# Products that nobody reads, in a score bank set aside, in the last ticks of a two-layer attention kernel

## The chip, the cores and the metric

The kernel runs on one core of a Trainium2 chip. The metric is the device time of one execution in microseconds (us); less is better. The median of three runs of the kernel before is 2475.11 us.

## The reference, cut to what matters

Sixteen sequences of 512 rows with 128 features pass through two layers. Each layer is a layer norm, then an attention and a feed-forward block that are added to the same input. The first attention has 16 heads of 64 with a causal mask. The second ("L1") has 8 heads with two score maps each, so 16 maps of 512x512 for a sequence, no mask, 8 features a map, rotary positions, and a norm of each head's result:

```python
xn = _layernorm(x)
x = x + _L0_attn_ref(xn, ...) + _L0_ffn_ref(xn, ...)
xn = _layernorm(x)
x = x + _L1_attn_ref(xn, ...) + _L1_ffn_ref(xn, ...)
# inside _L1_attn_ref
scores = jnp.einsum('bshd,bthd->bhst', q, k) * d ** (-0.25)
w = jax.nn.softmax(scores, axis=-1)
o = o1 - lam * o2
```

## The kernel before, in words

All five engines walk through one list of ticks (`clocks()`). In a tick each engine does the pieces that a fixed table gives it, in an order written out by hand. A sequence's first attention takes 32 ticks; its second attention follows 58 ticks after its start (`L1_AT`), beside the first attention of the next sequence. So TensorE has the products of two sequences at hand in nearly every tick. Three clocks (g for the first half of the work, h for the second half, k for the second half of the last sequence) run together until tick 519 and apart after it (`CLOCKS`). `late(g)` is true from g = 528, when no first attention is left: from there TensorE has only the end of sequence 14's second attention (clock h), the last sequence's projections (g = 528 to 532) and then the last sequence's second attention (clock k, from 538), with nothing of another sequence beside it.

The second attention of a sequence goes in steps of `l1_steps`. A step can hold a "top" (`second_tops`, product at L1768) and a "key" (`second_keys`, product at L1754). Both are a pair of bf16 products with 512 columns, one on the array's rows 0 to 47 (to 50 for keys), one on rows 64 to 111 (to 114), each into a score bank of its own. VectorE takes the row maximum of a top's two banks (`row_max1`, L1362); ScalarE takes the exponential of a key's two banks (`exp1`, L1044). There are 32 tops and 32 keys. The keys lag the tops by 13 steps for the last sequence (`KEY_LAG`), because a key needs the row maxima of its group as extra rows: TensorE turns them (L1739), ScalarE and VectorE split them in three (L1028, L1349 to L1354), and SyncE stores them by DMA (L766). So the last sequence has 13 steps with tops alone, 19 with both and 13 with keys alone. After each 8 keys come the value products of the group (`pv1`, L1721: 16 products in f32, shown as 32 instructions, on all rows of the array and 32 columns each), then the turning of the heads (L1585) and the head norm on VectorE and GpSimd (L1370 to L1393, L852, L854).

The score banks sc0 to sc5 (`SCB = 6`) are dealt in turn, in the order of `score_order()`, by `in_turn`. Before a product TensorE waits until the reader of the tile that had the bank before has read it (`bank_free`). Two further banks (pj0, pj1) serve all other products.

The last sequence's projections for rotary positions: TensorE waits for the layer norm's result, turns it (`xnT1`, L1585), ScalarE copies it (L947), TensorE multiplies it with four weights (`rq`, `rqs`, `rk`, `rks`; L1595), VectorE rotates and splits the results (L1330 to L1342), SyncE stores them (L742) and loads them stacked (L759); the first top waits for that.

Of the kernel before, what the change touches and what calls it, by code (L numbers as in the profile page):

```python
# [22 lines left out]
NB = 16  # L23
T = 512
D = 128
P = 128
# [26 lines left out]
STACK = SLOTS * DS  # L53
# [45 lines left out]
TICKS = 4 * NPAIR  # L99
# [52 lines left out]
VALUES_AT = (8, 8)  # L152
PJB = 2
SCB = 6

def l1_chunk(h, last, part=None):
# [94 lines left out]
def l1_steps(h, k, part=None):  # L252

    steps = []
    for n, clock in enumerate((h, k)):
        if clock is not None:
            i = Seq((clock - L1_AT) // TICKS)
            if i.live() and i.last() == (n == 1):
                steps.extend((i, t) for t in l1_chunk(clock, n, part))
    return steps  # L260
# [114 lines left out]
def score_order():  # L375

    order = []

    def second_keys(h, k, part):

        for i, t in l1_steps(h, k, part):
            if t >= KEY_LAG[i.last()]:
                order.extend(("st1", 2 * (t - KEY_LAG[i.last()]) + n, i.lo) for n in range(2))

    def second_tops(h, k, part):

        for i, t in l1_steps(h, k, part):
            if t < NU:
                order.extend(("mx1", 2 * t + n, i.lo) for n in range(2))

    def tops(g, lag, q):

        p, i = pair(g, lag)
        if i is not None:
            order.extend(("mx0", 6 * p + max(0, 2 * (q - 1)) + j, i.lo) for j in range(2))

    def turned(g, lag, group):

        p, i = pair(g, lag)
        if i is not None:  # L400
            order.extend(("tr0", 6 * p + 2 * group + n, i.lo) for n in range(2))

    for g, h, k in clocks():
        if g is not None and g % TICKS == 0:
            order.append(None)
        r = next(t for t in (g, k, h) if t is not None) % 4
        if late(g) and r == 0:
            second_keys(h, k, 0)
            tops(g, 0, 0)
            second_keys(h, k, 1)  # L410
            second_tops(h, k, 0)
            turned(g, 2, 1)
            second_tops(h, k, 1)
        elif late(g) and r == 1:
            second_tops(h, k, 0)
            turned(g, 2, 2)
            second_keys(h, k, 0)
            second_tops(h, k, 1)
            second_keys(h, k, 1)
        elif late(g) and r == 2:  # L420
            second_tops(h, k, 0)
            second_tops(h, k, 1)
            tops(g, 0, 2)
            second_keys(h, k, 0)
            tops(g, 0, 3)
            second_keys(h, k, 1)
        elif late(g) and r == 3:
            second_keys(h, k, 0)
            second_keys(h, k, 1)
            second_tops(h, k, 0)  # L430
            turned(g, 1, 0)
            second_tops(h, k, 1)
        elif r == 0:
            second_keys(h, k, 0)
            second_tops(h, k, 0)
            turned(g, 2, 1)
            tops(g, 0, 0)
            second_keys(h, k, 1)
            second_tops(h, k, 1)
        elif r == 1:  # L440
            turned(g, 2, 2)
            second_keys(h, k, 0)
            second_tops(h, k, 0)
            second_tops(h, k, 1)
            second_keys(h, k, 1)
        elif r == 2:
            tops(g, 0, 2)
            second_keys(h, k, 0)
            second_tops(h, k, 0)
            second_tops(h, k, 1)  # L450
            second_keys(h, k, 1)
            tops(g, 0, 3)
        else:
            second_keys(h, k, 0)
            second_tops(h, k, 0)
            turned(g, 1, 0)
            second_keys(h, k, 1)
            second_tops(h, k, 1)
    return order

def in_turn(order, banks):

    uses, of_bank, n = {}, [[] for _ in range(banks)], 0
    for use in order:
        if use is None:
            n = 0
            continue
        of_bank[n % banks].append(use)  # L470
        uses[use] = (n % banks, len(of_bank[n % banks]))
        n += 1
    return uses, of_bank
# [3 lines left out]
PJ_USES, _ = in_turn(PJ_ORDER, PJB)  # L477
TILES, TILES_OF = in_turn(score_order(), SCB)

def pj_use(seq, name):

    return PJ_USES.get((name, seq.lo), (0, 0))
# [29 lines left out]
def build_program(nc, a, out):  # L513
    ctx = ExitStack()
    with ctx:
# [52 lines left out]
        mx0 = sb("mx0", [P, NROWS, 8])  # L568
# [17 lines left out]
        QS = sb("QS", [P, H1, T], BF16)  # L586
        KS = sb("KS", [P, H1, T], BF16)
# [22 lines left out]
        pj = [ps(f"pj{n}") for n in range(PJB)]  # L610
        sc = [ps(f"sc{n}") for n in range(SCB)]

# [39 lines left out]
        reader = {"mx0": (s_mxd0, 8 * NPAIR), "tr0": (s_ev, N_TURN), "mx1": (s_mxd1, NS * NT), "st1": (s_exp1, NS * NT)}  # L652
# [918 lines left out]
        def _(pe):  # L1571
            pe.wait_ge(s_ld[0], NLOAD[0])
            used = []

            def bank(i, name):

# [134 lines left out]
            def pv1(i, g):  # L1711

                if g == 0:
                    b_, u = pj_use(i, "vals")
                    pe.wait_ge(s_pje[b_], u)
                t, full = bank(i, f"w{g}")
                for k in range(NT):
                    pe.wait_ge(s_exp1, i.upto(L1N, GS * (NT * g + k + 1)))
                    for j in range(GS):
                        unit = i.upto(NU, (GS * (NT * g + k) + j) // 2)  # L1720
                        last = pe.matmul(t[32 * j:32 * (j + 1), :], values1[i.last()][:, k, (GS * g + j) // 2, :],  # L1721
                                         pt1[:, 2 * (unit % UNITS) + j % 2, :], start=k == 0, stop=k == NT - 1)
                    if k < NT - 1:
                        last.then_inc(s_pv1, 1)
                last.then_inc(full, 1)
# [17 lines left out]
            def second_keys(h, k, part):  # L1743

                for i, t in l1_steps(h, k, part):
                    queries, keys = stacks[i.last()]
                    if (m := t - KEY_LAG[i.last()]) >= 0:
                        group, slot, k, _ = l1_key_pair(m)
                        if m % GU == 0:
                            pe.wait_ge(s_nd[group % 2], i.upto(96, 48 * (group // 2 + 1)))  # L1750
                        for n in range(2):
                            bank_free(i, "st1", 2 * m + n)
                            r = slice(HALF * n, HALF * n + STACK + 3)
                            pe.matmul(sc[tile_bank(i, "st1", 2 * m + n)][:, :], keys[r, slot, P * k:P * (k + 1)], queries[r, slot, :],  # L1754
                                      start=True, stop=True).then_inc(s_st1, 1)

            def second_tops(h, k, part):

                for i, t in l1_steps(h, k, part):
                    queries, keys = stacks[i.last()]  # L1760
                    if t == 0:
                        pe.wait_ge(s_stk, i.upto(64, 64))
                    if t < NU:
                        group, slot, q, _ = l1_max_pair(t)
                        for n in range(2):
                            bank_free(i, "mx1", 2 * t + n)
                            r = slice(HALF * n, HALF * n + STACK)
                            pe.matmul(sc[tile_bank(i, "mx1", 2 * t + n)][:, :], queries[r, slot, P * q:P * (q + 1)], keys[r, slot, :],  # L1768
                                      start=True, stop=True).then_inc(s_mxf1, 1)

            def second_values(h, k, part):

                for i, t in l1_steps(h, k, part):
                    if (group := l1_heads(i, t, VALUES_AT[i.last()])) is not None:
                        pv1(i, group)

            def others(g, h, k):

# [15 lines left out]
                if (i := at(g, XNT1_AT)) is not None:  # L1794
                    if i.first():
                        pe.wait_ge(s_vprep, N_VPREP)
                    pe.wait_ge(s_lnv[1], i.upto(24, 12))
                    transpose4(i, "xnT1", lambda k: xn[:, k, :])
                for w in range(2):
                    if (i := at(g, ROPE_AT[w])) is not None:  # L1800
                        if w == 0:
                            b_, u = pj_use(i, "xnT1")
                            pe.wait_ge(s_pje[b_], u)
                        for c, name in enumerate((("rq", "rqs"), ("rk", "rks"))[w]):
                            project(i, name, lambda k: w_l1[:, 2 * w + c, :], lambda k: xnT1[:, :], 1)
# [192 lines left out]
```

## Time and profile before

| | us |
|---|---|
| median of 3 runs (lowest, highest) | 2475.11 (2465.77, 2478.99) |
| the profiled execution, its own time | 2475.11 |
| its span | 2473.2 |
| TensorE / ScalarE / VectorE / GpSimd busy | 2349.1 / 1876.5 / 1832.7 / 1443.5 |
| TensorE's mean granted clock, share of 2.4 GHz | 0.982 |

The span is what the trace covers; 1.9 us of the profiled execution lie around it. A granted clock of 1.00 is 2.4 GHz, 0.50 is 1.2 GHz. TensorE's busy time counts from a product's start to its modelled end, so products that overlap are counted once, and a product that waits for a bank isn't busy.

### The profile page before, as it was taken

To read this page: it belongs to the slowest core of one execution; us is meant where nothing else is said; L and a number is where in the kernel's file an instruction comes from. 1 tells how busy PE (TensorE), PEld (TensorE's weight loads), DVE (VectorE), ACT (ScalarE), POOL (GpSimd) and SP (SyncE) were. 2 spreads that over 40 slices of the span, in tenths; PEclk is the share of its full clock that TensorE was granted. 3 is DMA by queue.
4 is the path that set the end of the run, shared out by engine and by line. 5 is a ranking of instruction groups with operands and counts; after the bars stand their busy time and mean duration, and the time that the engine had idled before them with its cause. 6 is when DMAs were issued, how large, how long until landed. Compare 5 with 4: busy or idle time off the path is not lost.

```text
span 2473.2 us, 82166 instructions
## 1 busy us (share of the span) xinstructions
PE 2349.1 (95%) x32896; PEld 1136.1 (46%) x32896; DVE 1832.7 (74%) x5637; ACT 1876.5 (76%) x4707; POOL 1443.5 (58%) x1356
## 2 busy tenths in 40 slices
PE   6999999999999999999999999999999999999877
PEld 3554444444544444444444544444444444544322
DVE  5568687787877778687787877778786887877674
ACT  4877877877778787877878777887777877787434
POOL 5975574756648466574756657475574756556201
PEclk9999999999999999999999999999999999999877
DMA  3011020200202020020201102020020201102020
GB/s 100 4 38 23 7 58 3 57 6 20 45 3 62 3 57 8 6 58 3 62 3 29 36 7 57 3 57 7 7 58 3 62 2 40 25 3 57 2 56 5
DMA packets 59946, 70.45 MB, mean 28 GB/s; under 512 B 11056, under 2 KB 55344, under 8 KB 56368
## 3 DMA queue, kind: packets, MB, share of 16 engines
q1 hardware_dynamic: 59568, 65.21, 11.4%
q8 instruction: 262, 4.29, 0.7%
q14 instruction: 116, 0.95, 0.1%
HBM read 35.04 MB, written 29.36 MB: 26 GB/s over the span
## 4 chain that ended last, share of the span: by engine, by line
PE 77%; DVE 16%; ACT 3%; issue 2%; DMA 1%; SPq 0%; POOL 0%; POOLq 0%; DVEq 0%; ACTq 0%
PE pj L1595 18%; PE pj L1691 12%; PE sc L1659 10%; PE pj L1721 10%; PE sc L1676 5%; PE sc L1768 5%; PE pj L1707 5%; DVE mx L1362 5%; PE pj L1615 5%; PE sc L1754 4%; DVE pq L1309 4%; PE pj L1585 3%; ACT pt L1044 1%; DVE y L1330 1%; DVE onrm L1372 1%
## 5 line engine op out<-in xcount | busy, mean ns | idle before, releaser
L845 POOL TENSOR_SCALAR pq<-pq,rsum 128x128 f32<-128x128 f32 (+3 forms) x1024 | 1151.8, 1139 | 772.8 <-DVE rsum L1316 771.2
L1362 DVE TENSOR_REDUCE mx<-sc 128x1 f32<-128x512 f32 x1024 | 644.1, 679 | 247.5 <-PE sc L1768 247.1
L996 ACT ACTIVATE pq<-pq,mx 128x128 f32<-128x128 f32 (+3 forms) x1024 | 569.8, 570 | 25.9 <-DVE mx L1309 25.7
L1044 ACT ACTIVATE pt<-sc 128x512 f32<-128x512 f32 x1024 | 543.9, 607 | 36.0 <-PE sc L1754 34.6
L1309 DVE CUSTOM_DVE_ANT_0 pq<-sc,relkey 128x128 f32<-128x128 f32 (+3 forms) x1024 | 448.5, 484 | 158.7 <-PE sc L1659 156.1
L1014 ACT ACTIVATE pt<-sc 128x512 f32<-128x512 f32 (+1 forms) x768 | 376.6, 535 | 162.3 <-PE sc L1676 159.5
L1659 PE MATMUL sc<-K,Q 64*128 64x128 f32 (+3 forms) x2048 | 362.5, 452 | 15.7 <-DVE mx L1309 9.4
L1691 PE MATMUL pj<-pt,v 128*32 128x512 f32 (+3 forms) x4096 | 303.8, 437 | 8.5 <-DVE y L1330 5.7
L1676 PEld LDWEIGHTS sc<-ident,pq 64*128 64x128 f32 x5120 | 200.1, 138 | 189.8 <-issue 99.7
L1595 PE MATMUL pj<-xnT,wqkv 128*32 128x512 f32 x2048 | 263.1, 606 | 4.0 <-ACT xnT L947 2.0
L1676 PE MATMUL sc<-ident,pq 64*128 64x64 f32 x5120 | 234.6, 227 | 7.4 <-DVE mx L1309 4.0
L1754 PE MATMUL sc<-QS,KS 51*128 51x512 bf16 x960 | 215.7, 383 | 20.4 <-ACT pt L1044 11.9
L1768 PE MATMUL sc<-KS,QS 48*128 48x512 bf16 x960 | 208.5, 385 | 17.4 <-DVE mx L1362 8.5
L1721 PE MATMUL pj<-pt,v 128*32 128x512 f32 x1920 | 224.1, 609 | 0.8 <-DVE y L1330 0.8
L996 ACT ACTIVATION_READ_ACCUMULATOR pq<-pq,mx 128x1 f32 x1024 | 213.1, 208 | 0.0
L1691 PEld LDWEIGHTS pj<-pt,v 128*32 128x32 f32 x4096 | 128.8, 110 | 163.3 <-issue 135.8
L1659 PEld LDWEIGHTS sc<-K,Q 64*128 64x128 f32 x2048 | 156.3, 189 | 80.7 <-issue 28.5
L1768 PEld LDWEIGHTS sc<-KS,QS 48*128 48x128 bf16 x960 | 52.2, 94 | 193.1 <-DVE mx L1362 57.4
L1595 PE MATMUL pj<-wqkv,xnT 128*32 128x128 f32 x4096 | 140.2, 278 | 0.0
L987 ACT ACTIVATE att<-pj 128x512 f32<-128x512 f32 x128 | 76.9, 600 | 74.3 <-PE pj L1691 72.6
L1595 PEld LDWEIGHTS pj<-wqkv,xnT 128*32 128x32 f32 x4096 | 105.5, 111 | 59.3 <-issue 58.2
L1021 ACT ACTIVATE oraw<-pj 128x512 f32<-128x512 f32 x64 | 38.2, 597 | 116.7 <-PE pj L1721 116.7
(117 smaller groups left out, 2836.7 us busy)
## 6 DMA issues: line engine op xcount, KB each, us to landing
scr_p<-y SPq DMA_DIRECT2D x160, 128.0 KB, 2.4
QS<-scr_p SPq DMA_DIRECT2D x30, 384.0 KB, 5.8
KS<-scr_p SPq DMA_DIRECT2D x30, 384.0 KB, 8.5
x_in<-in_L_attn_x SPq DMA_DIRECT2D x16, 256.0 KB, 2.9
scr_p<-tanh SPq DMA_DIRECT2D x32, 128.0 KB, 2.4
out_x<-xres SPq DMA_DIRECT2D x15, 256.0 KB, 2.3
QS<-nrow SPq DMA_DIRECT2D x180, 4.0 KB
wqkv<-in_L_attn_w_qkv SPq DMA_DIRECT2D x1, 1536.0 KB, 6.5
```

Source lines behind the costliest of these rows:

```text
L845: pool.tensor_scalar(rows, rows, rsum[:, row_slot(i, p), c:c + 1], None, ALU.mult).then_inc(s_scl, 1)
L996: act.activation(rows, rows, ACT.Exp, scale=-1.0, bias=mx0[:, row_slot(i, p), c:c + 1], accum_out=lsum[:, row_slot(i, p), c:c + 1]).then_i ...
L1014: act.activation(to[:, :, h, :], sc[tile_bank(i, "tr0", m)][:, 0:cols].rearrange("p (n c) -> p n c", c=HALF), ACT.Copy).then_inc(s_ev, 1)
L1044: act.activation(pt1[:, 2 * (unit % UNITS) + h, :], sc[tile_bank(i, "st1", 2 * n + h)][:, :], ACT.Exp, scale=float(DS) ** -0.25).then_inc( ...
L1309: dve.tensor_tensor_reduce(out=pq[:, at:at + width], in0=sc[tile_bank(i, "mx0", m)][:, left:left + width], in1=relkey[:, T - width:T], sca ...
L1362: dve.reduce_max(mx1[:, g % 2, at:at + 1], sc[tile_bank(i, "mx1", 2 * t + h)][:, :], AXIS.X).then_inc(s_mxd1, 1)
L1595: last = pe.matmul(t[r, c * k:c * (k + 1)], w(k)[:, r], x(k), start=True, stop=True)
L1659: last = pe.matmul(sc[tile_bank(i, "mx0", m + j)][:, left:left + width], Q0[r, b, P * row:P * (row + 1)], K0[r, b, 0:width], start=True, s ...
L1676: last = pe.transpose(sc[tile_bank(i, "tr0", m + h)][:, HALF * n:HALF * (n + 1)], pq[r, at:at + P], ident[r, r])
L1691: last = pe.matmul(t[r, P * k:T], v0[:, p % NBUF, k, r], pt[:, base:base + WIDTH[k]], start=k == 0, stop=k == NT - 1)
L1721: last = pe.matmul(t[32 * j:32 * (j + 1), :], values1[i.last()][:, k, (GS * g + j) // 2, :], pt1[:, 2 * (unit % UNITS) + j % 2, :], start= ...
L1768: pe.matmul(sc[tile_bank(i, "mx1", 2 * t + n)][:, :], queries[r, slot, P * q:P * (q + 1)], keys[r, slot, :], start=True, stop=True).then_i ...
```

## The change

A score bank, sc5, is set aside from g = 528 on: `score_order()` puts a mark there, and `in_turn` deals the five others from then on. `unread(n)` issues n bf16 products, each with 48 rows, 128 columns of weights and 512 columns of data from the old stacks QS and KS, into sc5. Nobody reads them and they signal nothing; the first call waits until the last reader of sc5 is done. Calls: 8 products before the wait for the last sequence's layer norm (`xnT1`), 3 before its first rotary projection, and 2 behind each of the last sequence's 32 tops and each of its 32 keys. That makes 11 and 128.

```diff
@@ tables
+UNREAD = (2, 2, 8, 3)
@@ score_order
+        if g == TICKS * NB + 16:
+            order.append(SET_ASIDE)
@@ in_turn
+        if use == SET_ASIDE:
+            banks -= 1
+            n = 0
+            continue
@@ second_keys, behind the pair of products
+                        if i.last():
+                            unread(UNREAD[0])
@@ second_tops, behind the pair of products
+                        if i.last():
+                            unread(UNREAD[1])
@@ new
+            def unread(products):
+
+                if not unread_begun:
+                    was, n, lo = TILES_OF[SCB - 1][-1]
+                    assert was != "mx0"
+                    done, per = reader[was]
+                    pe.wait_ge(done, Seq(lo).upto(per, n + 1))
+                    unread_begun.append(True)
+                for _ in range(products):
+                    pe.matmul(sc[SCB - 1][:, :], KS[0:STACK, 0, 0:P], QS[0:STACK, 0, :], start=True, stop=True)
@@ others
                 if (i := at(g, XNT1_AT)) is not None:
                     if i.first():
                         pe.wait_ge(s_vprep, N_VPREP)
+                    if i.last():
+                        unread(UNREAD[2])
                     pe.wait_ge(s_lnv[1], i.upto(24, 12))
                     transpose4(i, "xnT1", lambda k: xn[:, k, :])
                 for w in range(2):
                     if (i := at(g, ROPE_AT[w])) is not None:
                         if w == 0:
+                            if i.last():
+                                unread(UNREAD[3])
                             b_, u = pj_use(i, "xnT1")
                             pe.wait_ge(s_pje[b_], u)
```

## Rows read from the trace of the kernel before

**Rows 1.** The page: TensorE's share and its granted clock in 40 slices.
```profile
PE   6999999999999999999999999999999999999877
...
PEclk9999999999999999999999999999999999999877
```

**Rows 2.** Busy time by stage: span, each engine's busy us (instructions), granted clock, DMA.
```profile
1000.00:2200.00 1200.00, 1166.84 (x16735) 571.11 (x16731) 926.21 (x2853) 951.17 (x2391) 727.90 (x682) 1.00 0.12 27
2200.00:2345.00 145.00, 132.05 (x1737) 63.07 (x1729) 98.54 (x281) 97.36 (x236) 69.13 (x63) 0.95 0.11 26
2345.00:2379.00 34.00, 26.76 (x206) 9.76 (x206) 18.17 (x47) 12.12 (x24) 7.43 (x8) 0.76 0.46 101
2379.00:2400.00 21.00, 13.63 (x179) 5.46 (x177) 18.25 (x32) 4.54 (x9) 0.00 (x0) 0.89 0.01 1
2400.00:2473.20 73.20, 57.18 (x285) 15.88 (x285) 37.50 (x83) 35.74 (x72) 7.33 (x8) 0.69 0.02 5
```

**Rows 3.** The same view, the last second attention: groups of steps and value products, by turns.
```profile
2400.70:2411.70 11.00, 11.00 (x33) 2.28 (x33) 9.82 (x19) 8.33 (x17) 0.00 (x0) 0.50 0.01 3
2411.70:2417.30 5.60, 5.60 (x35) 1.29 (x36) 1.45 (x3) 0.39 (x1) 0.00 (x0) 0.65 0.00 0
2417.30:2431.10 13.80, 11.05 (x44) 2.93 (x43) 10.97 (x23) 8.68 (x18) 1.83 (x2) 0.69 0.01 1
2431.10:2437.10 6.00, 6.00 (x33) 1.29 (x32) 3.15 (x7) 0.26 (x1) 0.00 (x0) 0.58 0.01 3
2437.10:2443.90 6.80, 5.48 (x29) 1.63 (x25) 3.05 (x6) 6.06 (x14) 0.00 (x0) 0.93 0.00 0
2443.90:2448.70 4.80, 4.80 (x35) 1.09 (x34) 2.45 (x10) 2.40 (x5) 1.83 (x2) 0.74 0.01 3
2448.70:2455.30 6.60, 5.28 (x28) 1.75 (x26) 1.28 (x4) 6.12 (x13) 0.00 (x0) 0.84 0.00 0
2455.30:2459.60 4.30, 4.25 (x33) 0.96 (x32) 1.46 (x5) 2.31 (x5) 1.83 (x2) 0.85 0.00 0
```

**Rows 4.** TensorE in order of time: start, us, what, idle time before it.
```profile
2332.20 3.64 PE L1721 MATMUL pj<-pt,v 128*32 128x512 f32 x32
...
2357.83 0.82 PE L1754 MATMUL sc<-QS,KS 51*128 51x512 bf16 x6
...
2360.66 5.34 PE L1721 MATMUL pj<-pt,v 128*32 128x512 f32 x32 [0.82 <-DVE y L1330]
...
2378.81 0.39 PE L1768 MATMUL sc<-pq 48*128 48x512 bf16 x2
...
2400.69 1.03 PE L1754 MATMUL sc<-pq 51*128 51x512 bf16 x4 [3.15 <-DMA pq<-nrow]
...
2465.83 1.11 PE L1585 MATMUL pj<-ident,o 128*128 128x128 f32 x4 [4.90 <-DVE o L1393]
```

**Rows 5.** Groups by line between 2402 and 2412: busy us, mean ns.
```profile
L1362 DVE TENSOR_REDUCE mx<-sc 128x1 f32<-128x512 f32 x15 | 9.2, 682 | 0.8 <-PE sc L1768 0.8
...
L1754 PE MATMUL sc<-pq 51*128 51x512 bf16 x12 | 5.6, 611 | 0.0
```

**Rows 6.** The granted clock around the stop at 2397 and in the value products after it.
```profile
2398.00:2398.50 0.50, 0.00 (x0) 0.00 (x0) 0.50 (x2) 0.00 (x0) 0.00 (x0) 1.00 0.00 0
2399.00:2399.50 0.50, 0.00 (x0) 0.00 (x0) 0.50 (x2) 0.00 (x0) 0.00 (x0) 0.50 0.04 8
...
2415.50:2416.00 0.50, 0.50 (x8) 0.12 (x4) 0.00 (x0) 0.00 (x0) 0.00 (x0) 0.84 0.00 0
...
2402.00:2412.00 10.00, 10.00 (x33) 2.11 (x35) 9.38 (x18) 8.03 (x16) 0.00 (x0) 0.50 0.01 4
```

**Rows 7.** SyncE's queue and ScalarE in order of time, around the projections and the third group.
```profile
2366.36 2.47 SPq L759 DMA_DIRECT2D pq<-scr_p  x4
...
2352.32 1.08 ACT L1044 ACTIVATE pt<-sc 128x512 f32<-128x512 f32 x2
...
2439.29 4.05 ACT L1044 ACTIVATE pt<-sc 128x512 f32<-128x512 f32 x8
```

More of the change, by code:

```diff
@@ L459, in score_order @@
     return order
+SET_ASIDE = "set aside"
 def in_turn(order, banks):
@@ L1573, in _ @@
             used = []
+            unread_begun = []
             def bank(i, name):
```

## The prediction

> **What bounds the kernel now.** I read the page first: TensorE is busy nine tenths of every slice but the first and the last three, and only in those last three does its clock leave nine tenths [rows 1]. The stages put numbers to it: 1.00 over the long middle, 0.95, 0.76, 0.89 and 0.69 from 2200 us on [rows 2]. The change touches only what lies behind some 2350 us, so about 120 us; the others stay as they are, TensorE-bound at full clock.
>
> In the last second attention TensorE is rarely the bound while scores run. A step with a top and a key gives VectorE two reductions and ScalarE two exponentials. VectorE does its two in 2 x 0.61 us: 15 reductions busy 9.2 [rows 5], and the first eight steps take 11.0 us at a clock of 0.50 [rows 3]: 1.38 a step. Four exponentials take 2.03 (8 in 4.05), so a step with a key alone costs ScalarE 1.01 [rows 7]. The value products are different: TensorE alone sets their time, at 3.64 us with the full clock and at 5.6, 6.0, 4.8 and 4.3 in the tail [rows 3, 4]. There, in a few projections and in the last turns the low clock is paid for.
>
> **Prices.** Nothing in the trace runs on its own in a bank that nobody reads, but the unread product is a top's first product. At full clock three pairs take 0.82 us, and one, from start to end, 0.39; so a pair costs (0.82 - 0.39) / 2 = 0.215 [rows 4]. At half clock two pairs take 1.03 and one product 0.61: 0.42 a pair [rows 4, 5]. I take 0.43, twice the full-clock price. The two of a pair lie on different rows of the array and overlap. The unread ones all lie on rows 0 to 47, so each costs what a pair costs; the low bound, that they overlap with the pair's second product for nothing, is excluded for more than one of the two. A step with top and key then takes TensorE 6 x 0.215 = 1.29 us at full clock, 6 x 0.43 = 2.58 at half; before it was 0.43 and 0.86.
>
> **Does the clock stay up?** In the 3.15 us in which TensorE waits for the row maxima's DMA [rows 4] the clock falls from 1.00 to 0.50 [rows 6]. No unread product fills this wait: it stands at a key, and the unread ones stand behind keys. Then, from 2402 to 2412, TensorE has score products under way the whole time, 10.00 of 10 us busy, and the clock stays at 0.50 [rows 6]. It rises 3.9 us into the value products, which fill all 128 rows [rows 3, 6]. What went ahead of the rise was full-height work, and score work on 48 and 51 rows had gone on before it for 10 us without one. The unread products are more of that score work. I take it that they don't raise the clock from 0.50 either, but that they hold it at 1.00 once it is there: at full clock, score steps with a few turns between them had 0.93 from 2437 to 2444 [rows 3].
>
> The Trainium skill, page "TensorE: Matmul & The Clock Gate", section "Part 1: The HAM clock gate", says that activity of the array releases the throttle, and speaks of how busy TensorE is, not of how many rows are filled. By that rule the dense steps would bring the clock back; the trace, with 10.00 of 10 us busy at 0.50, does not bear it out. It is rival 1.
>
> **The sum,** against the profiled execution (2475.11, which is also the median).
> - 8 products before xnT1: 8 x 0.215 = 1.7 us; 3 before the projections: 0.65. Both lie on the path: I take the layer norm to be done before TensorE comes to wait for it, since the value products ahead of it take 5 to 6 us at half clock. ScalarE's two exponentials (1.08 [rows 7]) hide a part, the lost bank gives it back. +2.4. For it the value products at 2360.66 keep the full clock, 5.34 to 3.64 [rows 4]: -1.7. The stacks' loads, issued from 2366.36 [rows 7], move by 2.4 and should still land by the first top at 2378.81 [rows 4]. **+0.7** (bounds 0 and +4).
> - 13 steps with tops alone: 26 x 0.215 = 5.6 us of TensorE. It idles 21.0 - 13.6 = 7.4 there and VectorE is busy for 18.25 of 21 [rows 2], which covers it except ahead of the feed-forward projections. **+0.5** (-1 to +3).
> - First eight steps with both, at half clock: 8 x 2.58 = 20.6 against 11.0 [rows 3]: **+9.6**. If the clock were full all the time VectorE's 1.38 would go on: 0.
> - Their value products: still half clock at the start, 5.6 to 5.2: **-0.4**.
> - Second eight, now at full clock. VectorE is the bound with 10.97 busy in 13.8 [rows 3]; TensorE needs 10.3 and hides under it. A little idle time goes, but no tops are left over from the value products: **-0.8** (-2 to +3).
> - Their value products 6.0 to 3.6: **-2.4**.
> - Third eight, three with tops and five without: 3 x 1.29 + 5 x 0.645 + 0.9 for turns = 8.0, TensorE-bound, against 6.8: **+1.2**. Value products 4.8 to 3.6: **-1.2**.
> - Last eight, ScalarE-bound: one bank fewer leaves one exponential fewer (0.5) to be done under the value products: **+0.5**. Value products 4.3 to 3.9: **-0.4**.
> - The end: TensorE idles 4.90 for the head norm [rows 4], with no unread product there; clock and time as before: 0.
> - The set-aside bank in sequence 14's last steps: 0 to +1, inside the first line. The first call's wait is for a read that ended before the value products: 0, and otherwise ScalarE's 0.5.
>
> Sum: 0.7 + 0.5 + 9.6 - 0.4 - 0.8 - 2.4 + 1.2 - 1.2 + 0.5 - 0.4 = +7.3, so **2482 us**, +0.3%. A measurement of this kernel tells about 0.5% (12 us) from no change.
>
> **Rivals.**
> 1. The unread products do raise the clock (the page's rule). If it rises 3.9 us after 2400.7, as it does in the value products, 1.5 steps run at 2.58 and 6.5 at 1.38: 12.9 instead of 20.6, -7.7, and the first value products take 3.6, -1.6. 7.3 - 9.3 = -2.0: **2473 us**. For it: TensorE is then busy without a gap. Against: rows 6. Chance 0.24.
> 2. Slower: the clock falls again in the second eight steps, since TensorE stands there behind VectorE (busy 11.05 of 13.8, clock 0.69 [rows 3]) and once low it is not raised by score work. Then these take 8 x 2.58 + 0.9 = 21.5 instead of 13.0, +8.5, and their value products 5.5 instead of 3.6, +1.9: 7.3 + 10.4 = +17.7, **2493 us**. It decides where VectorE turns from reductions to the head norm and waits for GpSimd's part of it (1.83 busy [rows 3]). The steps with unread products fill TensorE better than those of before, which speaks against it. If the unread products do nothing for the clock at all, so that the change doesn't do what it says, this is the case too. Chance 0.17.
> 3. All of it works: the clock is full from 2350 on and no product costs anything. Then 1.7, the four value products' 20.7 - 14.6 = 6.1, and some 5 in the stages of 0.76 and 0.89 [rows 2] come off: **2462 us**. Against: 139 x 0.215 = 30 us of products have to hide, and the long waits stay, 3.15 and 4.90 among them [rows 4]. Chance 0.06.
>
> **How the numbers follow.** The forecast has 0.53; two in ten of it lie above +12. Slower by over 0.5%: 0.17 x 0.85 + 0.53 x 0.2 = 0.25. Faster: rival 3 and little else, 0.05. Within: 0.70. The forecast's own range is 2475 to 2490. The whole range takes in rival 1 with the spread of the runs shown (2466 to 2479) and most of rival 2: 2466 to 2493.
>
> **What would show it.** Right: the stretch from the first key to the first value products grows from 11 to about 20 us at 0.50, TensorE without idle time and VectorE starved; the second eight steps take 12 to 14 at about 1.00; the second value products take 3.6. The first top starts 0 to 2 us later than before. Wrong: the clock at 1.00 before 2408 or so (rival 1), or value products of 6 us behind 20 us of steps a second time (rival 2).

## The result, and the profile after

| | before | changed |
|---|---|---|
| median, us | 2475.52 | 2490.64 |
| lowest to highest | 2465.77 to 2478.99 | 2482.74 to 2495.07 |
| ratio, 95% interval | | 1.0063, 1.0045 to 1.0080 |

The change makes the kernel 15.1 us (0.6%) slower. In a second set of executions the ratio was 1.0070 (1.0051 to 1.0089). The profiled execution of the changed kernel is the one of 2482.74 us, its fastest; its span is 2480.9. The code up to tick 528 is the same in both kernels, so I compare from the start of the value products ahead of `xnT1`: 2345.5 us before, 2339.6 here. From there to the end it is 127.7 us before and 141.3 here, 13.6 more. That it came to that point 5.9 us sooner is no merit of the change, since the code ahead is shared: in the 79.6 us ahead of that point the granted clock was 0.96 here and 0.90 before.

The busy time by stage (the view of [rows 3], same columns), the changed kernel:

```profile
2345.10:2356.20 11.10, 10.23 (x70) 3.25 (x66) 6.67 (x14) 7.46 (x15) 1.84 (x2) 1.00 0.09 25
2356.20:2359.80 3.60, 3.60 (x32) 0.93 (x32) 3.36 (x6) 1.68 (x4) 0.00 (x0) 1.00 0.65 179
2359.80:2373.90 14.10, 6.09 (x90) 4.19 (x88) 5.79 (x18) 3.73 (x6) 1.84 (x2) 0.76 0.91 177
2373.90:2395.80 21.90, 17.57 (x205) 7.16 (x205) 18.33 (x32) 3.96 (x7) 0.00 (x0) 0.90 0.01 3
2395.80:2416.80 21.00, 21.00 (x65) 7.74 (x65) 11.25 (x21) 8.95 (x17) 0.00 (x0) 0.50 0.00 1
2416.80:2423.00 6.20, 6.20 (x35) 1.41 (x36) 0.56 (x1) 0.00 (x0) 0.00 (x0) 0.58 0.01 3
2423.00:2440.10 17.10, 14.59 (x73) 5.04 (x73) 13.49 (x28) 8.99 (x18) 1.83 (x2) 0.87 0.01 1
2440.10:2444.80 4.70, 4.70 (x33) 1.07 (x32) 0.80 (x2) 0.00 (x0) 0.00 (x0) 0.75 0.00 0
2444.80:2453.00 8.20, 7.83 (x50) 3.10 (x47) 3.99 (x9) 7.05 (x16) 0.00 (x0) 1.00 0.01 2
2453.00:2456.60 3.60, 3.60 (x35) 0.97 (x36) 1.38 (x5) 1.47 (x3) 1.83 (x2) 1.00 0.02 3
2456.60:2463.70 7.10, 6.63 (x44) 2.29 (x43) 1.66 (x6) 6.65 (x14) 0.00 (x0) 1.00 0.00 0
2463.70:2467.30 3.60, 3.60 (x33) 0.89 (x32) 1.25 (x5) 1.79 (x4) 1.83 (x2) 1.00 0.00 0
```

From the fifth line on these are the first eight steps with tops and keys, their value products, and so on in turns, as in [rows 3]. The first eight went from 11.0 to 21.0 us with TensorE busy for all 21.00 and the clock at 0.50. The last four stages have the full clock, and their value products the 3.60 that it gives. So in this execution the change does what it says at the end, and pays for it in the middle.

What a step is made of there: TensorE in order of time, the changed kernel (L1765 a key's product, L1781 a top's, L1801 an unread one).

```profile
2402.61 1.06 PE L1801 MATMUL sc<-QS,KS 48*128 48x512 bf16 x2
2403.46 0.63 PE L1781 MATMUL sc<-pq 48*128 48x512 bf16 x1
2403.56 0.60 PE L1765 MATMUL sc<-pq 51*128 51x512 bf16 x1
2403.89 1.06 PE L1801 MATMUL sc<-QS,KS 48*128 48x512 bf16 x2
...
2405.16 1.06 PE L1801 MATMUL sc<-QS,KS 48*128 48x512 bf16 x2
```

One pair of unread products follows the next in 1.28 us (2402.61, 2403.89, 2405.16), so a step with a top and a key takes 2.56. VectorE shows what that does to it, in order of time:

```profile
2404.13 1.29 DVE L1372 TENSOR_REDUCE mx<-sc 128x1 f32<-128x512 f32 x2 [1.27 <-PE sc L1781]
2406.69 1.29 DVE L1372 TENSOR_REDUCE mx<-sc 128x1 f32<-128x512 f32 x2 [1.27 <-PE sc L1781]
```

It works for 1.29 and waits 1.27 for TensorE, where before it waited 0.8 us in ten [rows 5].

### The profile page after: what moved, and what is told of

Same layout as the page of the kernel before. It is cut to its first block, busy times and chain, and to the rows that moved or that the text cites. A ratio compares the mean times of both kernels' runs of the same rounds, so it can differ in the third digit from the quotient of the medians.

```text
span 2480.9 us, 82444 instructions
## 1 busy us (share of the span) xinstructions
PE 2361.9 (95%) x33035; PEld 1143.0 (46%) x33035; DVE 1834.1 (74%) x5637; ACT 1878.7 (76%) x4707; POOL 1444.5 (58%) x1356
## 4 chain that ended last, share of the span: by engine, by line
PE 77%; DVE 16%; ACT 3%; issue 2%; DMA 1%; SPq 0%; POOL 0%; POOLq 0%; DVEq 0%; ACTq 0%
PE pj L1606 18%; PE pj L1702 12%; PE sc L1670 10%; PE pj L1732 9%; PE sc L1687 5%; PE sc L1781 5%; PE pj L1718 5%; DVE mx L1372 5%; PE pj L1626 5%; PE sc L1765 4%; DVE pq L1319 4%; PE pj L1596 3%; ACT pt L1054 1%; DVE y L1340 1%; PE sc L1801 1%
## 5 line engine op out<-in xcount | busy, mean ns | idle before, releaser
L1006 ACT ACTIVATE pq<-pq,mx 128x128 f32<-128x128 f32 (+3 forms) x1024 | 570.1, 570 | 27.1 <-DVE mx L1319 26.9
L1670 PE MATMUL sc<-K,Q 64*128 64x128 f32 (+3 forms) x2048 | 362.6, 452 | 15.7 <-DVE mx L1319 9.4
L1765 PE MATMUL sc<-QS,KS 51*128 51x512 bf16 x960 | 215.6, 383 | 20.9 <-ACT pt L1054 12.0
L1781 PE MATMUL sc<-KS,QS 48*128 48x512 bf16 x960 | 208.3, 384 | 18.3 <-DVE mx L1372 8.5
L1781 PEld LDWEIGHTS sc<-KS,QS 48*128 48x128 bf16 x960 | 52.0, 93 | 194.1 <-DVE mx L1372 57.5
L862 POOL TENSOR_SCALAR mse<-ms 128x8 f32<-128x8 f32 x64 | 12.9, 202 | 200.7 <-DVE ms L1390 198.3
```

The costliest lines, as they stand in the source:

```text
L1006: act.activation(rows, rows, ACT.Exp, scale=-1.0, bias=mx0[:, row_slot(i, p), c:c + 1], accum_out=lsum[:, row_slot(i, p), c:c + 1]).then_i ...
L1670: last = pe.matmul(sc[tile_bank(i, "mx0", m + j)][:, left:left + width], Q0[r, b, P * row:P * (row + 1)], K0[r, b, 0:width], start=True, s ...
```

## The experiments

**The change once more**, for a second profile. No edit.

> The changed kernel once more, for more executions and a second profile, whose falls of the clock lie elsewhere. My theory: first eight steps 21 us at 0.50 again, 2488 to 2492 us. Rival (the first profile was a lucky or unlucky one in these steps): 11 to 16 us there.

2493.52 us (2488 to 2492 was expected), ratio 1.0070. The first eight steps took 21.0 at 0.50 again. By stage:

```profile
2402.60:2423.60 21.00, 20.98 (x65) 7.74 (x65) 11.25 (x21) 8.95 (x17) 0.00 (x0) 0.50 0.00 1
...
2428.60:2445.70 17.10, 13.49 (x73) 4.77 (x71) 13.51 (x28) 8.99 (x18) 1.83 (x2) 0.93 0.01 1
2445.70:2451.50 5.80, 5.80 (x35) 1.33 (x36) 0.79 (x2) 0.00 (x0) 0.00 (x0) 0.61 0.00 0
2451.50:2462.00 10.50, 10.13 (x49) 3.76 (x45) 4.92 (x12) 8.33 (x18) 1.08 (x2) 0.76 0.01 3
2462.00:2468.20 6.20, 6.20 (x35) 1.38 (x36) 0.87 (x3) 0.44 (x1) 0.75 (x1) 0.58 0.00 0
```

The first and second eight steps are the same to 0.1 us. What differs is the third eight and their value products, 10.5 and 6.2 instead of 8.2 and 3.6. The clock came back in the second value products, as in the first profile, but fell again at 2457.0:

```profile
2453.00:2457.00 4.00, 3.63 (x21) 1.06 (x19) 1.53 (x3) 4.00 (x10) 0.00 (x0) 1.00 0.02 4
2457.00:2462.00 5.00, 5.00 (x18) 1.98 (x17) 2.30 (x8) 3.95 (x10) 1.08 (x2) 0.50 0.01 2
```

TensorE was busy for 3.63 of the 4 us ahead of that fall, with keys, a top and the unread products behind them. So these products don't hold the clock at 1.00 either; in the first profile it stayed up through the same steps. This execution reached the value products ahead of `xnT1` at 2346.0, as the kernel before did, and took 146.6 from there, 18.9 more. The two profiles give 13.6 and 18.9; the medians lie 15 and 19 apart.

**The bank alone.** Five banks, no unread product.

```diff
-UNREAD = (2, 2, 8, 3)
+UNREAD = (0, 0, 0, 0)
```

> The bank is set aside, no unread product is issued. My theory (the unread products at half clock make TensorE the bound of the first eight steps with tops and keys): the bank alone costs 0 to 2 us, 2475 to 2478 us, and the first eight steps take 11 us as in the kernel before. Rival (one bank fewer starves VectorE and ScalarE): most of the 15 us are here, 2485 us or more.

2484.04 us, ratio 1.0023 (1.0011 to 1.0034), which is 6 us (7 between the medians): neither "0 to 2" nor "most of it". The first eight steps took 11.6 (11.1 before). The second eight took 16.3 instead of 13.8:

```profile
2418.40:2434.70 16.30, 12.20 (x42) 3.11 (x42) 12.94 (x28) 9.07 (x18) 1.83 (x2) 0.63 0.00 1
```

TensorE is idle for 4.1 us of it (2.75 before) and busy for 12.2 (11.05 before). The clock is 0.63 (0.69 before). The longest waits are for VectorE, which is in the head norm:

```profile
2431.09 0.60 PE L1781 MATMUL sc<-pq 48*128 48x512 bf16 x1 [1.65 <-DVE mx L1372]
...
2434.15 0.61 PE L1781 MATMUL sc<-pq 48*128 48x512 bf16 x1 [1.43 <-DVE mx L1372]
```

With five banks TensorE stops twice at a top and can't go on to the value products; before it stopped once (1.65). The third value products took 6.3 instead of 4.8, with the clock at 0.58. I had priced the bank at nothing up to 1, and 0.5 in the last eight steps.

**The eleven at the projections**, with the bank, nothing behind tops and keys.

```diff
-UNREAD = (2, 2, 8, 3)
+UNREAD = (0, 0, 8, 3)
```

> The bank set aside and the eleven products at the projections, nothing behind tops and keys. Against the kernel with the bank alone: the stacks' transfers start 1.5 to 2.4 us later, so it takes 1 to 3 us longer, 2484 to 2487 us. Rival (the eleven keep the clock up through the value products behind them and pay for themselves): 2480 to 2483.

2485.14 us, ratio 1.0032 (1.0018 to 1.0046), in the middle of what was expected; against the bank alone, 1 to 2 us more, and the intervals overlap. The stretch between the value products ahead of `xnT1` and the next ones (2360.66 in [rows 4]) takes 11.1 us (9.6 with the bank alone, 9.0 before). Those next value products take 3.6 with the bank alone too, so the eleven products are not what keeps the clock up there. In all seven profiles with five score banks they take 3.6, in all seven with six 5.3. So the bank's being set aside goes with it; by what way is open.

**No unread products behind keys.**

```diff
-UNREAD = (2, 2, 8, 3)
+UNREAD = (0, 2, 8, 3)
```

> As the changed kernel, but nothing unread behind the 32 keys (64 products fewer). My theory: a step with top and key takes TensorE 4 x 0.43 = 1.72 us at half clock instead of 2.58, so the first eight take 14 instead of 21 us; the whole is 2479 to 2482 us. Rival (it is the fall at the head norm that costs, not the first eight steps): 2488 to 2491.

2487.50 us, ratio 1.0039 (1.0025 to 1.0053). The first eight steps took 14.6 at 0.50, near the 14 of the price list (8 x 1.72 = 13.8, and a turn). The whole came out some 6 us above what I expected. In the profile the second eight took 18.2 at a clock of 0.62, and the third and fourth value products 5.4 and 4.4, where the changed kernel's first profile has 17.1, 3.6 and 3.6:

```profile
2402.70:2417.30 14.60, 14.59 (x53) 4.59 (x56) 11.16 (x21) 8.45 (x17) 0.00 (x0) 0.50 0.01 1
2422.10:2440.30 18.20, 15.10 (x61) 4.65 (x57) 13.43 (x28) 8.89 (x18) 1.83 (x2) 0.62 0.01 2
```

So with fewer products the clock was low for more of the second eight, and the ones that are left cost double there. It is one profile, so how much of the 6 us this is remains open.

**One unread product behind each top and key.**

```diff
-UNREAD = (2, 2, 8, 3)
+UNREAD = (1, 1, 8, 3)
```

> One unread product behind each top and key instead of two. My theory: a step takes 4 x 0.43 = 1.72 us at half clock, the first eight 14 us, and the clock falls more often elsewhere; 2480 to 2484 us. If time went with the number of products alone (64 fewer), it would lie half way, 2483; if the clock rose in time, as with two products it did not, below 2476.

2489.16 us, ratio 1.0035 (1.0014 to 1.0056): the ratio is what "half way" gives, the median is above the 2480 to 2484 expected. The ten times run from 2475.85 to 2495.08, too wide to say more. The profile has the first eight steps at 14.3 and 0.50, as expected.

**Full-height unread products.** Same number, same columns, but on 128 rows.

```diff
-                    pe.matmul(sc[SCB - 1][:, :], KS[0:STACK, 0, 0:P], QS[0:STACK, 0, :], start=True, stop=True)
+                    pe.matmul(sc[SCB - 1][:, :], KS[:, 0, 0:P], QS[:, 0, :], start=True, stop=True)
```

> As the changed kernel, but each unread product takes all 128 rows of KS and QS instead of 48; its time is the same. My theory (score-height products keep the clock where it is, full-height ones raise it): the clock rises about 4 us into the first eight steps, which take 13 us instead of 21, and it doesn't fall at the head norm; 2474 to 2480 us. Rival (TensorE being busy or not decides, rows don't matter): the first eight steps stay at 0.50 and 21 us, 2488 to 2491.

2488.44 us, ratio 1.0036 (1.0021 to 1.0051). The first eight steps by stage, and the two microseconds in which the clock rose:

```profile
2409.20:2425.50 16.30, 16.15 (x64) 3.53 (x65) 10.77 (x20) 8.55 (x17) 0.00 (x0) 0.83 0.01 1
...
2429.10:2448.80 19.70, 17.27 (x75) 4.48 (x73) 14.06 (x29) 9.20 (x18) 1.83 (x2) 0.92 0.00 1
...
2414.00:2415.00 1.00, 1.00 (x4) 0.13 (x2) 0.78 (x3) 0.00 (x0) 0.00 (x0) 0.56 0.00 0
2415.00:2416.00 1.00, 1.00 (x7) 0.28 (x6) 1.00 (x3) 0.00 (x0) 0.00 (x0) 1.00 0.00 0
```

The clock came back 5 to 6 us into the steps, where with 48 rows it stayed away for 21: the theory about the rows holds for the rise, the rival is out. The clock did fall again in the second eight (0.92), and the forecast of the time, 2474 to 2480, doesn't hold. With full-height products TensorE needs 1.72 a step even at full clock, 0.86 for a pair and its two:

```profile
2417.65 0.39 PE L1765 MATMUL sc<-pq 51*128 51x512 bf16 x2
2417.98 0.61 PE L1801 MATMUL sc<-QS,KS 128*128 128x512 bf16 x2
2418.51 0.39 PE L1781 MATMUL sc<-pq 48*128 48x512 bf16 x2
...
2419.37 0.39 PE L1765 MATMUL sc<-pq 51*128 51x512 bf16 x2
```

**The products without the bank.** Six banks; the first product of each pair is issued three times into its own bank; nothing at the projections.

```diff
                             r = slice(HALF * n, HALF * n + STACK + 3)
+                            for _ in range(2 if i.last() and n == 0 else 0):
+                                pe.matmul(sc[tile_bank(i, "st1", 2 * m + n)][:, :], keys[r, slot, P * k:P * (k + 1)], queries[r, slot, :],
+                                          start=True, stop=True)
...
```

(The same in `second_tops`.)

> Six score banks as before, no products at the projections; the first product of each of the last sequence's pairs is issued three times into its own bank, so that TensorE's work behind the first top is that of the changed kernel (128 products more). My theory by now has two parts, products and bank: the first eight steps take 21 us at 0.50 as in the changed kernel, the second eight 14 to 15 instead of 17; some 6 us less than the changed kernel, 2482 to 2486 us. Rival (the bank costs nothing beside the products): 2489 to 2491.

2490.64 us, ratio 1.0061 (1.0044 to 1.0078). The time is the rival's: giving the bank back gained nothing that shows.

```profile
2404.90:2425.90 21.00, 21.00 (x65) 6.85 (x65) 10.51 (x19) 8.82 (x17) 0.00 (x0) 0.50 0.00 1
...
2432.10:2447.80 15.70, 13.73 (x73) 5.65 (x72) 12.17 (x26) 8.99 (x18) 1.83 (x2) 0.90 0.01 1
...
2453.30:2464.00 10.70, 10.32 (x45) 3.93 (x43) 4.87 (x12) 7.68 (x16) 0.95 (x2) 0.74 0.01 3
```

The second eight took 15.7, which is 1.4 less than in the changed kernel (14 to 15 was expected), and the third 10.7, near the 10.5 of its second profile. The bank's 6 us and the products' 15 don't add up to what the changed kernel lost, though intervals of 4 us to either side leave room for a part of the 6. The products alone are enough for a loss of the same size.

**Towards a version that gains.** Four kernels with six score banks. The first two set one of the two other banks aside (pj1, behind the last feed-forward block) and put full-height products in it: 14 in the wait ahead of the first key, one behind each key, and in the first kernel also one behind each top from the ninth on.

```diff
+ASIDE_AT = TICKS * (NB - 1) + 64
+FILL = (1, 1, 14)
...
+                for _ in range(products):
+                    pe.matmul(pj[1][:, :], KS[:, 0, 0:P], QS[:, 0, :], start=True, stop=True)
```

> Against the kernel before: six score banks, one of the two other banks set aside behind the last sequence's feed-forward block instead, 14 unread full-height products in the wait ahead of the first key, and one unread full-height product behind each key and each top from the ninth on. My theory: the clock stays at 1.00 through the wait and the steps, which VectorE bounds at 1.4 us, the four value products take 3.6 us each instead of 5.6, 6.0, 4.8 and 4.3; 4 to 7 us less than before, 2469 to 2473 us. Rival (TensorE becomes the bound with these products in its order too): 2477 to 2483.

> As the one before, without the unread products behind tops. My theory: less work for TensorE, and the clock may fall once in the steps; if it holds, 2469 to 2473 us, if it falls in the first eight steps 2473 to 2477. Rival (the full-height products behind keys are too few to matter): 2475 to 2478.

2477.60 us, ratio 1.0003 (0.9991 to 1.0015), and 2477.64, ratio 1.0007 (0.9995 to 1.0019): no difference to the kernel before, and both where the rivals had put them. The first of the two by stage:

```profile
2402.90:2414.60 11.70, 11.53 (x50) 3.38 (x49) 9.98 (x20) 8.45 (x17) 0.00 (x0) 1.00 0.01 2
...
2418.20:2433.90 15.70, 13.43 (x63) 3.92 (x59) 12.28 (x26) 9.10 (x18) 1.83 (x2) 0.92 0.01 2
2439.60:2449.60 10.00, 8.33 (x39) 2.49 (x35) 4.96 (x12) 7.41 (x16) 0.29 (x2) 0.94 0.01 1
```

The first eight steps now have the full clock and take 11.7, where before they took 11.1 at half of it; their value products take 3.6 instead of 5.6. (In the second kernel, with nothing behind tops, the clock fell again at about 2405.3, within those steps, and the value products took 4.6.) But the second eight take 1.9 more and the third 3.2 more, with the clock at 0.92 and 0.94. I didn't separate whether that is the bank or the products.

The other two set nothing aside. Each product is issued twice into its own bank (keys and, in the first, tops from the ninth on), so that both halves of the rows are filled, and 14 pairs fill the wait ahead of the first key.

```diff
+TWICE = (1, 1, 14)
...
+                            for _ in range(TWICE[0] if i.last() else 0):
+                                pe.matmul(sc[tile_bank(i, "st1", 2 * m + n)][:, :], keys[r, slot, P * k:P * (k + 1)], queries[r, slot, :],
+                                          start=True, stop=True)
                             pe.matmul(sc[tile_bank(i, "st1", 2 * m + n)][:, :], keys[r, slot, P * k:P * (k + 1)], queries[r, slot, :],
```

> Against the kernel before, no bank is set aside: each product of the last sequence's keys, and of its tops from the ninth on, is issued twice into its own bank, so both rows halves of the array work and a pair costs 0.43 us at full clock; 14 pairs fill the wait ahead of the first key. My theory (the clock follows how much of the array the score work fills, and unread work is free only while VectorE or ScalarE is the bound): the clock holds through the first steps, the value products take 3.6 to 4.6 us, a few us less than before, 2470 to 2474. Rival (later real products cost VectorE and ScalarE what the clock gives back, as with the unread products in the other bank): 2475 to 2481.

> As the one before with the tops issued once. My theory: less cost in the steps, the clock falls once or twice; 2471 to 2475. Rival: 2475 to 2480.

2479.80, ratio 1.0018 (1.0005 to 1.0031), and 2478.73, ratio 1.0013 (1.0001 to 1.0025): slightly slower, and again with the rivals. The filling pairs came late, behind a wait for a bank, and at half clock:

```profile
2399.76 6.16 PE L1755 MATMUL sc<-pq 48*128 48x512 bf16 x28 [1.54 <-DVE mx L1363]
```

The stage of tops grew by 4.5 us to 26.4. But the clock then stood at 1.00: it rose at about 2406.0, 6.2 us after these pairs began. So the last kernel is this one without the 14 pairs:

```diff
-TWICE = (1, 1, 14)
+TWICE = (1, 1, 0)
```

> As the kernel with the pairs issued twice, without the 14 pairs ahead of the first key, which began late, at half clock, and took 6.2 us where 1.5 of waiting were left. My theory: the wait ahead of the first key is again short, the clock is at 0.50 at the first key and comes back within the first eight steps, since both halves of the rows are filled without a gap (1.72 us a step until then); the first eight take 12 to 13 us, their value products 3.6; the whole 4 us less than with the 14, 2473 to 2476, no different from before. Rival (it takes full-height work to raise the clock): the first eight take 14 us at 0.50, 2477 to 2480.

2475.89 us, ratio 1.0001 (0.9989 to 1.0013): the kernel before, neither better nor worse. Its first key starts at 2399.2 with the clock at 0.50, and the steps raise it:

```profile
2399.20:2411.40 12.20, 12.19 (x65) 4.37 (x65) 9.65 (x18) 8.37 (x17) 0.00 (x0) 0.81 0.01 3
2415.10:2430.00 14.90, 13.25 (x73) 3.94 (x71) 11.71 (x26) 8.94 (x18) 1.83 (x2) 0.92 0.01 2
...
2402.00:2403.00 1.00, 1.00 (x6) 0.43 (x4) 1.00 (x2) 0.39 (x1) 0.00 (x0) 0.50 0.00 0
...
2404.00:2405.00 1.00, 1.00 (x6) 0.21 (x3) 1.00 (x3) 0.72 (x2) 0.00 (x0) 1.00 0.00 0
```

Score products alone, none of full height, brought the clock back 4 to 5 us after they began. In the changed kernel TensorE was just as busy and it stayed at 0.50 for 21 us. What differs in those microseconds is that the doubled products lie on both halves of the rows and the unread ones on one. More products are under way in a microsecond too, eight in 1.72 us against eight in 2.56, but that rival is out: with the unread ones on 128 rows it was eight in 3.02 at half clock (2409.18 to 2412.20), and the clock rose. The rival of this run, that full height is needed, is out, and so is that part of my own wording.

The stages side by side, in us, each from one profile (first key, and the starts and ends of the L1721 products of `pv1`; the last column runs from the value products ahead of `xnT1` to the end of the span):

| kernel | tops | 8 steps | values | 8 | values | 8 | values | 8 | values | all |
|---|---|---|---|---|---|---|---|---|---|---|
| before | 21.9 | 11.1 | 5.6 | 13.8 | 6.1 | 6.7 | 4.8 | 6.5 | 4.3 | 127.7 |
| changed | 21.9 | 21.0 | 6.2 | 17.2 | 4.8 | 8.1 | 3.6 | 7.0 | 3.6 | 141.3 |
| changed, again | 21.8 | 21.0 | 4.9 | 17.1 | 5.8 | 10.5 | 6.2 | 7.0 | 3.6 | 146.6 |
| bank alone | 23.0 | 11.6 | 4.6 | 16.3 | 6.1 | 7.2 | 6.3 | 7.0 | 4.8 | 134.3 |
| six banks | 21.0 | 21.0 | 6.2 | 15.7 | 5.5 | 10.7 | 5.9 | 6.7 | 3.7 | 143.6 |
| full height | 23.0 | 16.3 | 3.6 | 19.7 | 5.4 | 9.2 | 3.6 | 7.5 | 3.6 | 140.6 |
| pairs twice, no filling | 22.1 | 12.2 | 3.6 | 15.0 | 5.8 | 7.2 | 3.6 | 7.6 | 3.9 | 128.3 |

## Why the prediction was right and where it was wrong

The measured 2490.6 lies in the range of 2466 to 2493, 8.6 above the 2482 forecast. "Within 0.5%" had 0.70 and did not come, by 1.0063 (the interval takes in 0.5%); "slower" had 0.25. The forecast's own range ended at 2490, so the measured time is in the whole range thanks to rival 2. By stretches: up to the first key +1.2 was forecast and +1.0 and +1.4 came, in the two profiles; the first eight steps +9.6, and +10.0 both times; everything behind them -3.5, and +2.6 and +7.5. The first half of the mechanism was right. The gain that was to follow it did not come.

- **The price of a step and the clock in it** held: 8 x 2.58 = 20.6 was forecast, 21.0 measured, twice, at 0.50 for its whole length. This is +10.0 of the 13.6 and of the 18.9 in the two profiles, the largest single part of the loss. The reason given, that unread products are only more score work, was right for these products and too wide as a rule (see the last run). The row it rested on was weaker than it was taken to be: two pairs need 0.86 of a step's 1.38 us at half clock, so the 10.00 of 10 us busy was not a test of dense work.
- **The Trainium skill's** rule on the throttle (page "TensorE: Matmul & The Clock Gate", section "Part 1: The HAM clock gate"), that how busy the engine has been sets its clock, was rival 1. The trace disagrees: 21.00 of 21 us busy at 0.50.
- **That the unread products hold the clock at 1.00 once it is there** did not come out either. In the first profile it fell at 2391.2, among the tops, with TensorE busy for 2.6 of the 3 us ahead; in the second at 2457.0, with 3.6 of 4. The long wait that the prediction blamed was 1.15 us instead of 3.15 in both (2395.80 in the first), and the clock had fallen before it.
- **The second eight steps** were the step that failed: "VectorE is the bound ...; TensorE needs 10.3 and hides under it. A little idle time goes, but no tops are left over from the value products: -0.8". They took 17.1, not 13.0, with VectorE busy for 13.5 of it and not for 10.97. The larger of two engines' work is not the length of such a stretch. VectorE starts with nothing and waits for TensorE at first; later TensorE waits for VectorE's head norm. VectorE, the changed kernel, in order of time:

```profile
2423.34 3.89 DVE L1372 TENSOR_REDUCE mx<-sc 128x1 f32<-128x512 f32 x6 [5.98 <-PE sc L1781]
2428.54 2.48 DVE L1372 TENSOR_REDUCE mx<-sc 128x1 f32<-128x512 f32 x4 [1.32 <-PE sc L1781]
```

and TensorE, in the same steps:

```profile
2436.11 0.61 PE L1781 MATMUL sc<-pq 48*128 48x512 bf16 x1 [1.87 <-DVE mx L1372]
```

  The larger part is at the end of the stretch. These are VectorE's last four reductions in it, before and changed:

```profile
2431.84 2.48 DVE L1362 TENSOR_REDUCE mx<-sc 128x1 f32<-128x512 f32 x4
```

```profile
2438.43 2.48 DVE L1372 TENSOR_REDUCE mx<-sc 128x1 f32<-128x512 f32 x4
```

  From its first reduction of the stretch to the last VectorE took 16.7 us before (from 2417.66) and 17.6 here (from 2423.34), 0.9 more. But before TensorE began the value products 3.2 us ahead of VectorE's end (2431.08 and 2434.32), and here 0.8 (2440.13 and 2440.91). That makes the other 2.5. With the bank alone the value products begin 1.2 us ahead of that end, with six banks and the products 2.1. So work of VectorE that had lain beside the value products came onto the path, and the missing bank has the larger share in it.
- **The value products** of these steps took 4.7 and 5.8, not 3.6, because the clock fell ahead of them: in the first profile at 2435.6, in that wait, in the second at 2443.4, as a second wait of 1.42 us began. That is the place that rival 2 names ("where VectorE turns from reductions to the head norm"), and these 1.1 to 2.2 us are its. The 4.1 in the steps are not: they took 17.1 in both profiles, though the clock fell with 4.5 us left in one and 2.3 in the other. The measured time lies between forecast and rival 2, in part for another reason than rival 2's.
- **The set-aside bank** at "0 to +1", and +0.5 in the last eight steps, was mis-sized: alone it costs 6 us. That six banks gave nothing back that shows in the run with the products speaks for an overlap of the two. How, is open.
- **The eleven products**: +2.4 was forecast on the path and 2.1 came (9.0 to 11.1), 0.6 of it with the bank alone. The gain behind them came too, 5.3 to 3.6, but the bank alone has it, so the products didn't earn it. And the stacks' loads didn't land in time:

```profile
2373.88 0.39 PE L1781 MATMUL sc<-pq 48*128 48x512 bf16 x2 [1.27 <-DMA pq<-scr_p]
```

  From the end of the first value products to the first top it is 28.8 instead of 27.1, +1.7 where +0.7 was forecast, inside its bounds.
- **Tops, last eight steps, the end**: 0, +0.5 and 0, against +0.5, +0.5 and 0. **First value products**: +0.6 and -0.6, against -0.4. **Last ones**: -0.7, against -0.4. **Third eight**: 8.2 where 8.0 was forecast in one profile, 10.5 in the other, with the clock at 0.50 from 2457.0 on. Their value products took 3.6 in the one, as forecast, and 6.2 in the other.
- **Rival 3** was out by far, and the four kernels meant to come near it show why: the most that a kept clock gave back was 2.0 in the first value products (5.6 to 3.6), 1.2 in the third and 0.7 in the last, and the steps around them grew by as much.

## What to carry to other kernels

Work added to keep TensorE's clock up is priced at the low clock first, since it is there that it has to act; here a step went from 0.86 to 2.56 us and past the 1.38 that VectorE had set. Look at what in the trace stood ahead of each rise, not just at whether the engine was busy, and let the added work resemble that: on both halves of the rows, or on all. Even so none of the kernels here with added work was faster than the one without. And where two engines take turns at being late, add up their waits instead of taking the larger sum, and ask which work had run beside the next stage and will no longer.

## What the runs showed of the hardware that was not expected

- TensorE busy without a gap does not bring the clock back by itself. Two pairs of score products and four more on the lower rows alone (0 to 47, or 50) in 2.56 us: 0.50 for 21 us, in three profiles. Score products on both halves, issued twice or as filling pairs: from 0.50 to 1.00 in 4 to 6 us. Unread ones on 128 rows: in 5 to 6.
- Nor does it hold it: the clock fell with TensorE busy for 2.6 of the 3 us ahead of the fall, and for 3.6 of 4, with the same products.
- A product on 128 rows behind a pair on halves costs more than its own 0.215 us: two of them and a pair take 0.86 at full clock (2417.65 to 2418.51), not 0.65.
- The same code ahead of the change ends between 2339.6 and 2353.0 us in the profiles in hand, and the clock falls at other places in each. A difference of 10 us between two single profiles of this kernel says nothing; the stretch from a common point says more, though it too was 141.3 and 146.6 us in two profiles of one kernel.
